# A graph network kernel: the node stage between its two passes over the edges, redistributed over the engines

## The reference, cut to what matters

```python
h = jnp.maximum(_layernorm(x, axis=-1), 0.0)
x = x + _L0_gnn_ref(h, edge_index, W, att_src, att_dst, bias)    # attention, 4 heads of 32
h = jnp.maximum(_layernorm(x, axis=-1), 0.0)
x = x + _L1_gnn_ref(h, edge_index, edge_attr_64, W1, b1, W2, b2)
return x

# _L0_gnn_ref: h = (x @ W.T) per head; w = softmax over the edges of a target
out = segment_sum(h[src] * w, dst);  return out.reshape(N, 128) + bias
# _L1_gnn_ref:
msg = concatenate([x[row], x[col], edge_attr])
h = relu(msg @ W1 + b1);  out = segment_sum(h @ W2 + b2, row)
```

## Time and profile before

| | us |
|---|---|
| Median of three timed runs | 5693.36 (5691.43 to 5695.14) |
| The profiled execution, its own time | 5693.23 |
| Its span in the trace | 5691.4 |
| TensorE busy | 5079.6 (89%) |
| VectorE busy | 3961.3 (70%) |
| GpSimd busy | 3874.4 (68%) |
| ScalarE busy | 2970.2 (52%) |

### The profile page before, as it was taken

One profiled execution on the slowest core, in us unless ns is written; L12 is line 12 of the kernel. 1 busy time (PEld: TensorE's weight loads), 2 busy tenths in 40 slices (PEclk: granted clock), 3 DMA queues, 4 the chain that ended last, 5 costly groups with the idle time before them and its releaser, 6 DMA issues.

```text
span 5691.4 us, 159502 instructions
## 1 busy us (share of the span) xinstructions
PE 5079.6 (89%) x33692; PEld 4021.1 (71%) x33693; DVE 3961.3 (70%) x14408; ACT 2970.2 (52%) x8485; POOL 3874.4 (68%) x3713
## 2 busy tenths in 40 slices
PE   4788888888888886999999999999997999999999
PEld 3677777777777774676666667666665887777787
DVE  6777878878887886555555555545545888888887
ACT  3566666666666663333333333333224777777776
POOL 4777777777777774677777777777776555555553
PEclk6888988888888887999999999999998999999999
DMA  4422222222222234998888888888886998999997
GB/s 110 164 54 52 54 53 53 53 53 53 53 53 54 53 107 138 283 273 266 264 261 258 264 262 261 264 260 260 260 262 185 222 223 219 216 218 220 219 222 190
DMA packets 859992, 994.46 MB, mean 175 GB/s; under 512 B 307993, under 2 KB 663225, under 8 KB 859776
## 3 DMA queue, kind: packets, MB, share of 16 engines
q1 hardware_dynamic: 662496, 610.19, 39.4%
q0 software_dynamic: 190592, 379.87, 23.7%
q10 hardware_dynamic: 6816, 3.38, 0.2%
HBM read 728.41 MB, written 264.62 MB: 174 GB/s over the span
## 4 chain that ended last, share of the span: by engine, by line
PE 57%; issue 11%; POOL 10%; DMA 9%; DVE 8%; DVEq 3%; ACT 2%; POOLq 0%; ACTq 0%; SPq 0%
PE bank L1705 13%; PE bank L1538 10%; PE bank L1628 8%; PE bank L1630 7%; PE bank L1695 7%; DMA xr<-arena 6%; POOL xr L547 5%; POOL arena L499 4%; PE bank L1464 2%; DMA arena<-h_tab,arena 2%; DVE arena L1055 2%; DVE arena L945 2%; PE bank L1618 1%; PE bank L1686 1%; DVE arena L1035 1%
## 5 line engine op out<-in xcount | busy, mean ns | idle before, releaser
L499 POOL DMA_INDIRECT arena<-h_tab,arena x1612 | 1560.4, 968 | 545.8 <-issue 405.6
L547 POOL DMA_INDIRECT xr<-arena x1612 | 1569.6, 974 | 511.8 <-issue 358.2
L1538 PE MATMUL bank<-arena 128*128 128x136 f32 x6448 | 1317.0, 333 | 73.7 <-DVE arena L1055 9.4
L719 ACT ACTIVATE arena<-bank 128x256 f32<-128x256 f32 x1612 | 593.9, 385 | 1388.4 <-PE bank L1630 963.7
L1628 PE MATMUL bank<-arena 128*128 128x256 f32 x3224 | 1023.2, 399 | 91.4 <-ACT arena L719 45.1
L1538 PEld LDWEIGHTS bank<-arena 128*128 128x128 f32 x6448 | 987.1, 215 | 158.4 <-DVE arena L1055 60.8
L561 POOL DMA_INDIRECT arena<-p_tab,arena x428 | 670.2, 1566 | 628.8 <-DMA arena<-p_tab,arena 503.4
L626 ACT ACTIVATE arena<-bank 128x256 bf16<-128x256 bf16 x1612 | 615.3, 382 | 799.1 <-PE bank L1464 714.6
L1630 PE MATMUL bank<-arena 128*128 128x256 f32 x3224 | 970.9, 383 | 0.0
L1705 PE MATMUL bank<-arena 128*128 128x257 f32 x3424 | 899.2, 385 | 7.3 <-issue 3.2
L1055 DVE TENSOR_TENSOR arena<-arena,bank 128x272 f32 x1612 | 694.6, 431 | 184.9 <-PE bank L1538 154.1
(11 more groups left out here) (255 smaller groups left out, 6481.6 us busy)
## 6 DMA issues: line engine op xcount, KB each, us to landing
arena<-xr SPq DMA_DIRECT2D x428, 520.0 KB
arena<-q_tab SPq DMA_DIRECT2D x1612, 128.0 KB
arena<-in_edge_attr SPq DMA_DIRECT2D x61, 832.0 KB
arena<-rel_tab SPq DMA_DIRECT2D x124, 224.0 KB
arena<-h_tab,arena POOLq DMA_INDIRECT x1612
xr<-arena POOLq DMA_INDIRECT x1612
arena<-rel_tab SPq DMA_DIRECT2D x124, 192.0 KB
xr<-arena SPq DMA_DIRECT2D x26, 520.0 KB
```

The lines of the kernel that those rows point to most:

```text
L499: pool.indirect_dma_start(G[:, q, t, :], None, h_tab, bass.IndirectOffsetOnAxis(ap=idx[:, q, t:t + 1], axis=0)).then_inc(sem(f"gath{q}"), 16)
L547: pool.indirect_dma_start(xr, bass.IndirectOffsetOnAxis(ap=pos[:, q, t:t + 1], axis=0), Rb[:, t, :], None).then_inc(sem(f"scat{m}"), 16)
L1538: last = pe.matmul(PSB[3 + t % 2][:, k * H * MW:(k + 1) * H * MW], OH[:, (t + 2 * q) % 4, k * P:(k + 1) * P], flat(msg[:, t, :, :]), start ...
```

## The change

GpSimd keeps one pass: it adds the bias to the loaded x, in place, with no wait for VectorE. VectorE computes the attention output itself (`attended`), then sum and negated mean; its `scales` makes the reciprocal of the root and the shift, and its `turned` copies the transposed tiles out of PSUM, which ScalarE did. ScalarE squares tile by tile, with the mean as bias and the sum as a side output, and makes `h2` tile by tile with relu, scale and shift. The order is by steps: at step k VectorE does the first part of chunk k, the scales of k-1 and the copies of k-2; ScalarE the relu of k-1, the squares of k, the product copies of k-2; TensorE the transposes of k-1, the products of k-2. SyncE's loop stays as it is, but for the block of windows, which moves from c = 5 to c = 4. The preparation of the first edge batch is spread over other steps.

```diff
--- before.py
+++ after.py
@@ -188,8 +188,9 @@
         pout = Region(X0 + PW)([HID])
         S = Region(X0, X0 + PW - NT * P)
         hs, xi, tt, x1c = (S([2, NC, D]) for _ in range(4))
-        sqm = h2 = S([NC, D])
-        den, rec, m7, v7 = S([NT, H]), S([NT, H]), S([NC]), S([NC])
+        h2 = S([NC, D])
+        den, rec = S([NT, H]), S([NT, H])
+        negm, vsum, sdev, rinv, shift = (S([2, NC]) for _ in range(5))
         Qst = S([2, NC, HID])
 
 
@@ -395,7 +396,7 @@
                     load_nodes(c + 2)
                 if c:
                     store_q(c - 1)
-                if c == 5:
+                if c == 4:
                     sp.wait_ge(sem("node_prep"), 2)
                     load_windows(0, 0, first=True, more="next")
             store_q(NCH - 1)
@@ -512,26 +513,11 @@
             with pool.Fori(1, NB // 2) as i:
                 for q in range(2):
                     gather(i, q)
-            pool.wait_ge(sem("acc_done"), 1 + NB * (BT + 1))
-            pool.wait_ge(sem("expanded"), NB * BT)
             pool.wait_ge(sem("w1_in"), 16 * 8)
-            hv = lambda v: v.rearrange("p n (h o) -> p n h o", h=H)
-            wide = lambda v: v.unsqueeze(3).to_broadcast([P, NC, H, DH])
             for c in range(NCH):
-                a = acc[:, c * NC:(c + 1) * NC, :].rearrange("p n (h m) -> p n h m", h=H)
-                t1, h = tt[:, c % 2, :, :], hs0 if c < 2 else hs
-                if c >= 2:
-                    pool.wait_ge(sem("h2_ready"), c - 1)
+                v = (xi0 if c < 2 else xi)[:, c % 2, :, :]
                 pool.wait_ge(sem(f"hs_in{c % 2}"), 32 * (c // 2 + 1) + (16 if c == NCH - 1 else 0))
-                M.tensor_tensor(hv(t1), hv(h[:, c % 2, :, :]), wide(a[:, :, :, DH + 1]), ALU.mult).then_inc(sem("t_step"), 1)
-                pool.wait_ge(sem("t_step"), 3 * c + 1)
-                M.tensor_tensor(hv(t1), hv(t1), a[:, :, :, 0:DH], ALU.add).then_inc(sem("t_step"), 1)
-                pool.wait_ge(sem("t_step"), 3 * c + 2)
-                if c == 0:
-                    pool.wait_ge(sem("node_prep"), 1)
-                M.tensor_tensor(hv(t1), hv(t1), wide(rec[:, c * NC:(c + 1) * NC, :]), ALU.mult).then_inc(sem("t_step"), 1)
-                pool.wait_ge(sem("t_step"), 3 * c + 3)
-                M.tensor_tensor(t1, t1, biasB.unsqueeze(1).to_broadcast([P, NC, D]), ALU.add).then_inc(sem("t_ready"), 1)
+                M.tensor_tensor(v, v, biasB.unsqueeze(1).to_broadcast([P, NC, D]), ALU.add).then_inc(sem("t_ready"), 1)
 
 
             pool.wait_ge(sem("filled"), 16 * (NFILL + NT))
@@ -739,27 +725,33 @@
                 act.wait_ge(sem("pq_ps"), u + 1)
                 A.activation(flat(Qst[:, c % 2, 2 * k:2 * k + n, :]), PSB[2 + u % 3][:, 0:n * HID], ACT.Copy).then_inc(sem("hi_ready"), 1)
 
-            counts_out(0)
-            for c in range(NCH + 1):
+            def squares_of(c):
+                act.wait_ge(sem("mean_ready"), c + 1)
+                for j in range(NC):
+                    last = A.activation(tt[:, c % 2, j, :], x1c[:, c % 2, j, :], ACT.Square, bias=negm[:, c % 2, j:j + 1],
+                                        accum_out=vsum[:, c % 2, j:j + 1])
+                last.then_inc(sem("sqm_ready"), 1)
+                act.wait_ge(sem("sqm_ready"), c + 1)
+                A.activation(sdev[:, c % 2, :], vsum[:, c % 2, :], ACT.Sqrt, bias=eps, scale=1.0 / D).then_inc(sem("s_ready"), 1)
+
+            def normal(c):
+                act.wait_ge(sem("rinv_ready"), c + 1)
                 if c:
-                    q_rows(c - 1, 0)
-                if c < NCH:
-                    act.wait_ge(sem("t_cent"), c + 1)
-                    if c:
-                        act.wait_ge(sem("h2T_ps"), c)
-                    A.activation(sqm, tt[:, c % 2, :, :], ACT.Square).then_inc(sem("sqm_ready"), 1)
-                if c:
-                    q_rows(c - 1, 1)
-                if c < NCH:
-                    act.wait_ge(sem("v_sum"), c + 1)
-                    A.activation(m7, v7, ACT.Sqrt, bias=eps, scale=1.0 / D).then_inc(sem("s_ready"), 1)
-                if c:
-                    q_rows(c - 1, 2)
-                    q_rows(c - 1, 3)
-                if c < NCH:
-                    act.wait_ge(sem("h2T_ps"), c + 1)
-                    A.activation(flat(h2T[:, c * NC:c * NC + 4, :]), PSB[0][:], ACT.Copy)
-                    A.activation(flat(h2T[:, c * NC + 4:(c + 1) * NC, :]), PSB[1][:, 0:(NC - 4) * P], ACT.Copy).then_inc(sem("h2T_ready"), 1)
+                    act.wait_ge(sem("h2T_ps"), c)
+                for j in range(NC):
+                    last = A.activation(h2[:, j, :], x1c[:, c % 2, j, :], ACT.Relu, bias=shift[:, c % 2, j:j + 1], scale=rinv[:, c % 2, j:j + 1])
+                last.then_inc(sem("h2_ready"), 1)
+
+            for k in range(NCH + 2):
+                if 1 <= k <= NCH:
+                    normal(k - 1)
+                if k < NCH:
+                    squares_of(k)
+                if k == 0:
+                    counts_out(0)
+                if k >= 2:
+                    for u in range(NQ):
+                        q_rows(k - 2, u)
             targets(0, 0, first=True, part=0)
             targets(1, 1, part=1)
             with act.Fori(1, NT // 2) as i:
@@ -1177,27 +1169,38 @@
             link(V.tensor_scalar(den, den, 1e-30, None, ALU.max))
             V.reciprocal(rec, den).then_inc(sem("node_prep"), 1)
 
-            def node(c):
-
-                t1, x1, v = tt[:, c % 2, :, :], x1c[:, c % 2, :, :], xi0 if c < 2 else xi
+            heads = lambda v: v.rearrange("p n (h o) -> p n h o", h=H)
+            wide = lambda v: v.unsqueeze(3).to_broadcast([P, NC, H, DH])
+
+            def attended(c):
+
+                a = acc[:, c * NC:(c + 1) * NC, :].rearrange("p n (h m) -> p n h m", h=H)
+                t1, x1 = tt[:, c % 2, :, :], x1c[:, c % 2, :, :]
+                h, v = (hs0, xi0) if c < 2 else (hs, xi)
+                dve.wait_ge(sem(f"hs_in{c % 2}"), 32 * (c // 2 + 1) + (16 if c == NCH - 1 else 0))
+                link(V.tensor_tensor(heads(t1), heads(h[:, c % 2, :, :]), wide(a[:, :, :, DH + 1]), ALU.mult))
+                link(V.tensor_tensor(heads(t1), heads(t1), a[:, :, :, 0:DH], ALU.add))
+                link(V.tensor_tensor(heads(t1), heads(t1), wide(rec[:, c * NC:(c + 1) * NC, :]), ALU.mult))
                 dve.wait_ge(sem("t_ready"), c + 1)
-                dve.wait_ge(sem(f"hs_in{c % 2}"), 32 * (c // 2 + 1) + (16 if c == NCH - 1 else 0))
                 if c >= 2:
                     dve.wait_ge(sem(f"x1_out{c % 2}"), 16 * (c // 2))
+                    dve.wait_ge(sem("h2_ready"), c - 1)
                 V.tensor_tensor(x1, t1, v[:, c % 2, :, :], ALU.add).then_inc(sem("x1_ready"), 1)
                 dve.wait_ge(sem("x1_ready"), c + 1)
                 if c == NCH - 3:
                     V.memset(xi[96:P, c % 2, NC - 1, :], 0.0).then_inc(sem("xi_pad"), 1)
-                link(V.tensor_reduce(v7, x1, AX.X, ALU.add))
-                link(V.tensor_scalar(v7, v7, 1.0 / D, None, ALU.mult))
-                V.tensor_tensor(t1, x1, v7.unsqueeze(2).to_broadcast([P, NC, D]), ALU.subtract).then_inc(sem("t_cent"), 1)
-                dve.wait_ge(sem("sqm_ready"), c + 1)
-                V.tensor_reduce(v7, sqm, AX.X, ALU.add).then_inc(sem("v_sum"), 1)
+                link(V.tensor_reduce(negm[:, c % 2, :], x1, AX.X, ALU.add))
+                V.tensor_scalar(negm[:, c % 2, :], negm[:, c % 2, :], -1.0 / D, None, ALU.mult).then_inc(sem("mean_ready"), 1)
+
+            def scales(c):
                 dve.wait_ge(sem("s_ready"), c + 1)
-                link(V.reciprocal(v7, m7))
-                if c:
-                    dve.wait_ge(sem("h2T_ps"), c)
-                V.scalar_tensor_tensor(h2, t1, 0.0, v7.unsqueeze(2).to_broadcast([P, NC, D]), ALU.max, ALU.mult).then_inc(sem("h2_ready"), 1)
+                link(V.reciprocal(rinv[:, c % 2, :], sdev[:, c % 2, :]))
+                V.tensor_tensor(shift[:, c % 2, :], negm[:, c % 2, :], rinv[:, c % 2, :], ALU.mult).then_inc(sem("rinv_ready"), 1)
+
+            def turned(c):
+                dve.wait_ge(sem("h2T_ps"), c + 1)
+                V.tensor_copy(flat(h2T[:, c * NC:c * NC + 4, :]), PSB[0][:])
+                V.tensor_copy(flat(h2T[:, c * NC + 4:(c + 1) * NC, :]), PSB[1][:, 0:(NC - 4) * P]).then_inc(sem("h2T_ready"), 1)
 
             def bins_of(r, s, first=False):
                 hi = hiE[:, bass.ds(r * BT, BT)]
@@ -1303,23 +1306,28 @@
                                     dve.wait_ge(sem(f"scat{m}"), 16 * psize[m] * b)
                             places(r, s)
             link(V.tensor_copy(bin_ps, iota[:, 0:NT]))
-            bins_of(0, 0, True)
-            for c in range(NCH):
-                node(c)
-                if c == 0:
-                    for m in range(3):
-                        rank(0, m)
-                        own(0, 0, m)
-                if c == 1:
-                    total(0)
-                if c == 2:
```

(40 more changed lines are left out.)

## The result

Over eleven executions each on one chip the changed kernel takes **5708.75 us** (5703.59 to 5719.83), the kernel before 5694.12 (5689.60 to 5700.74): ratio **1.0024**, 95% interval 1.0016 to 1.0032. So it is slower, just over what a measurement can tell from no change, where "no change that shows" was forecast (5698.5, range 5683 to 5707).

A forecast was written before the change was run, and what follows sets the result against it. The node stage was taken as a chain of waits with no engine full. Chunk turns, late loads and q(4)'s late store put its end +5.3 us later: 5693.23 + 5.3 = 5698.5 us, range 5683 to 5707.

The forecast's parts named there:

- rival A: Node stage: chunks get shorter where no load is awaited, late loads give it back; +5.3 us; chance 0.62.
- D: ScalarE's tables: relu or square in another set than the root, two loads a chunk, +23 us; chance 0.04.
- B: Node stage faster: loads are no wait or TensorE keeps its clock, -3 to -9 us; chance 0.18.
- Q(0): Moment ScalarE has copied out chunk 0's products; forecast at 2222.9 us, 1.3 earlier than before.
- Q(2): Moment ScalarE has copied out chunk 2's products; forecast at 2249.0 us.
- Q(3): Moment ScalarE has copied out chunk 3's products, behind which the moved block starts; forecast at 2258.7 us.
- Q(4): Moment ScalarE has copied out chunk 4's products; forecast at 2275.4 us.
- Q(6): Moment ScalarE has copied out chunk 6's products; forecast at 2288.9 us against 2283.6 before, +5.3.
- W: A ScalarE turn from the scales through relus, transposes, products and last copy: 9.0 us (6.3 fast, 9.9 slow).
- Exclusion: VectorE and GpSimd passes reading SBUF block each other: 2.1 us lost in each of chunks 0, 4, 6.
- rival C: Slower: moved block delays q(4)'s store, holding up chunk 6's copies; time +13 us; chance 0.16.
- The stage behind starts as before: After the node stage: the next stage is unchanged, so only the node stage's +5.3 us enters the time.

The follow-up runs named there:

- the first experiment: The changed kernel, unaltered, run again on another chip beside the kernel before: 5712.32 us, ratio 1.0015.
- The run with both edits: Changed kernel with loads ahead of the q stores in SyncE's queue and the block of windows behind q(4) again: 5699.83 us, ratio 0.9992.

## Why the prediction was wrong

**What bounds the kernel, and rival A**: right. The stage is a chain of waits, and the two that the forecast named came: VectorE idle ahead of chunks 4 and 6, released by the load of x, SyncE's block early (2264.41 against 2271.03), ScalarE waiting for q(4), seven adds with the first two at 2143. There was one table load in the stage (1.28 at 2203.41, for the first root), so D is out; all timed medians of the changed order lie above before's, so is B.

**The stage's length**: nearly exact in the first profile, by terms that were not. Counted from VectorE's first instruction (2186.8 before, 2189.96 here):

| | forecast | measured |
|---|---|---|
| Q(0) | 36.1 | 35.4 |
| data of chunk 4 behind Q(0) | 8.7 | 9.5 |
| Q(2) | 62.2 | 62.7 |
| data of chunk 6 behind Q(2) | 9.0 | 10.4 |
| Q(3) | 71.9 | 70.2 |
| Q(4) | 88.6 | 90.4 |
| q(4) landed | 100.2 | 100.2 |
| Q(6) | 102.1 | 102.0 |

Passes (1.12), transposes and products at either clock, and the q store's landing as the last step were as costed. **Mis-sized terms**: the seven relus take 2.80, one each 0.385, where 1.4 was put in from the plain copies of 128 words; the squares with their sums 2.8, not 2.1. In these turns W had 9.0, and the higher clock in some of them paid for it. The block's register loads between the q(3) store and the first issue, 3.9 us (2260.50 to 2264.41), were left out, and stood in the trace of before in the same place. On the other side Q(3) came 1.7 early, the block itself took 16.1 and not 16.8, and the store of q(4) landed 9.7 behind the block's end (2280.46 to 2290.12), where 11.1 was read from before. That these cancelled is luck.

**Exclusion**: put at 2.1 in each of three chunks, measured 1.75 (2.84 for a pass of 1.09), and in chunk 0 another 0.66 where the small product L1193 took 0.83 and ended with GpSimd's add. In chunk 4 VectorE's first pass started 0.04 before the add, the add took 2.97 instead of 2.07, and then VectorE's second pass waited for the add's end. The Trainium skill, page SBUF — State Buffer, section Who interferes with whom, calls the lock on the two engines' shared ports exclusive and says that the issue order decides who blocks; the trace agrees, in both directions, with 0.9 us lost by GpSimd and 1.75 by VectorE.

**The point estimate** is off by less in the stage than it looks: +5.3 forecast, +6.9 in four profiles. ScalarE's wait for q(4) is what varies: 2.57, 5.41, 4.39, 6.18 us, where the forecast let it cost 1.6. That is rival C's place. C was priced as an accident of a low clock, 4 us late; but the old kernel with nothing but the moved block waits 7.69 us and loses 7.8. So the first step that failed is the one that put the moved block at 1.6 us on the path and gave C its own 0.16 beside A: A's late loads and C's late store hang on one queue, and both waits came in each of the four profiles.

**The step that put the time outside the range** is the sentence "The stage behind starts as before": the sum adds nothing behind Q(6), and the high end, 5707, allows late turns in the node stage and nothing else. With the stage's +6.9 alone the time would have been about 5701, inside the range; measured is +14.6. Outside the node stage the four profiles of each kernel differ by 9.2 us in the last stage and by 0.3 ahead of the node stage. One profile of before was taken as the base and no spread was put on it, where the spans of four range over 8 us (5691.4 to 5699.8). The cause of this remaining part isn't shown, and on the chip of the first experiment, with +9.5 us in all, little of it is left.

**What the forecast missed altogether** is what the queue's order was worth. It treated the late loads as a price of the new steps. The run with both edits shows, in one profile, that the steps give 12 us in the stage and the order takes 19; by medians the order is worth 12.5.

## What to carry to other kernels

When work is regrouped into steps that lag a chunk, write out again each in-order queue that carries both loads and stores: a store that now waits a chunk longer holds back every load behind it. Two such delays can hide each other, so that undoing one shows almost nothing (3.7 and 1.4 us) where undoing both shows 12.5. Look behind the stage as well before a block of loads is moved back: one that was early enough before can be late for the next stage now (6.4 us). Price a small instruction from the nearest row with the same operands, a scale and a bias per partition included, and not from a plain copy. And take the base and its spread from several profiles before a range is closed around one stage.

## What the runs showed that was not expected

- **GpSimd's gathers are 7 to 8 ns longer when its program holds large adds.** 952 against 944 to 945 ns (medians of 1612), from the first gather at 76 us on, 2 ms ahead of the first add. An add of eight words at the end or seven memsets in the place of the adds leave them short. How the later adds reach the earlier gathers isn't settled: the size of the adds, their place and number, and how the program lies in memory weren't told apart. The aggregation ends 10.6 us earlier without them, most of what the best kernel (the bias as VectorE's fifth pass, 0.9964) gains beyond the reordered one (0.9992).
- **Relus of 128 words with scale and bias per partition take 0.385 us back to back**, squares with a sum 0.385 including the read of the accumulator (0.19), so a square with its sum costs no more than a relu.
- **TensorE's clock scatters between executions of the same stage.** Seven transposes take 0.98 us at full clock and 1.75 at the low one. In the kernel without bias they took 1.75 or 1.76 in six of seven chunks, with the eight-word add at the very end of the program in two of seven, and their node stages are 84.3 and 77.0 us. A difference of a few us in the stage between single profiles says little.

Transposes of chunk 3, without bias and then with the eight-word add (start, us, line, operation, shapes, count, idle before):

```profile
2226.43 1.76 PE L1575 MATMUL bank<-arena 128*128 128x128 f32 x7 [3.21 <-ACT arena L742]
```

```profile
2226.07 0.98 PE L1576 MATMUL bank<-arena 128*128 128x128 f32 x7 [3.21 <-ACT arena L743]
```

The idle time ahead of them is the same, 3.21. The granted clock isn't: 0.50 of full speed (1.2 GHz) over the first seven and 1.00 (2.4 GHz) over the second. Ahead of that pause the engine had done the same 14 products, in 5.40 us in the first case and in 4.84 in the second.
